# Reciprocal square roots of two normalisations on GpSimd (power) instead of ScalarE root and VectorE reciprocal

## What is computed

```python
def attn(x):                       # 16 heads of 32
    qf, kf = fft(x @ W_q.T per head), fft(x @ W_kv.T per head)
    qf, kf = qf / norm(qf), kf / norm(kf)      # norm of a head's 32 complex numbers
    v = real(ifft(qf * cumsum(kf, over rows)))
    return v @ W_o.T
x = x + attn(layernorm(x))
z = layernorm(x)
g = silu(z @ gate_w(fp8) * gate_scale) * (z @ up_w(fp8) * up_scale)    # 1536 wide
x = x + (g @ down_w(fp8)) * down_scale
```

## Time and profile before

| what | value |
|---|---|
| median of 3 runs | 439.82 us |
| profiled execution, its own time | 439.65 us |
| its span (first to last instruction) | 437.8 us |
| outside the span | 1.85 us |
| TensorE (PE) busy | 425.1 us, 97% |
| VectorE (DVE) busy | 276.2 us, 63% |
| ScalarE (ACT) busy | 185.2 us, 42% |
| GpSimd (POOL) busy | 104.9 us, 24% |

### The profile page before, as it was taken

The page is one execution under the profiler, slowest core; times in us unless marked ns, Lnnn a source line. Parts: engine busy times, 40 slices in busy tenths (PEclk is TensorE's granted clock), DMA queues, the critical chain, the costliest instruction groups (busy, mean ns, idle before and its releaser), DMA issues.

```text
span 437.8 us, 5468 instructions
## 1 busy us (share of the span) xinstructions
PE 425.1 (97%) x1976; PEld 280.2 (64%) x1976; DVE 276.2 (63%) x488; ACT 185.2 (42%) x299; POOL 104.9 (24%) x107
## 2 busy tenths in 40 slices
PE   4999999999999999999999999999999999999995
PEld 4886678745665676665565767666566666555554
DVE  5899889988797882347684571536865754523134
ACT  4958446873434542236432252434523243213130
POOL 0406620011745010400563311400254200400002
PEclk9999999999999999999999999999999999999999
DMA  7993490010240000250000100140000000200002
GB/s 215 328 293 117 141 304 4 0 49 2 72 155 15 1 2 0 85 156 0 2 0 2 49 1 1 47 146 0 0 2 1 1 0 1 96 1 1 0 0 97
DMA packets 17595, 26.14 MB, mean 60 GB/s; under 512 B 1824, under 2 KB 8224, under 8 KB 17568
## 3 DMA queue, kind: packets, MB, share of 16 engines
q1 hardware_dynamic: 17280, 25.77, 18.2%
q10 hardware_dynamic: 288, 0.02, 0.0%
HBM read 21.57 MB, written 4.19 MB: 59 GB/s over the span
## 4 chain that ended last, share of the span: by engine, by line
PE 93%; DMA 2%; POOL 2%; ACT 1%; DVE 1%; issue 0%; SPq 0%; DVEq 0%; POOLq 0%
PE bd L383 20%; PE bg L367 19%; PE bu L367 19%; PE ba L290 15%; PE ba L324 8%; PE bd L290 3%; PE ba L333 1%; PE bd L324 1%; PE ba L303 1%; PE ba L312 1%; DMA hT<-w_q_dram 1%; DMA xTr<-xT_dram 1%; PE bd L276 1%; PE bu L290 1%; PE bg L290 1%; POOL xTs L1350 1%
## 5 line engine op out<-in xcount | busy, mean ns | idle before, releaser
L383 PE MATMUL bd<-dw,fu 128*128 128x512 f32 x376 | 98.6, 406 | 0.0
L367 PE MATMUL bg<-hT,gu 128*128 128x512 f16 x384 | 91.1, 380 | 0.0
L367 PE MATMUL bu<-hT,gu 128*128 128x512 f16 x384 | 90.7, 379 | 0.0
L383 PEld LDWEIGHTS bd<-dw,fu 128*128 128x128 f32 x376 | 69.8, 188 | 16.1
L1046 DVE SCALAR_TENSOR_TENSOR ff<-bu,us,sl 128x512 f32<-128x512 f32 x48 | 35.9, 749 | 61.8 <-PE bu L367 59.8
L290 PE MATMUL ba<-wf,xTs 128*128 128x512 f32 x288 | 69.5, 395 | 0.0
L645 ACT ACTIVATE sl<-bg,gs 128x512 f32<-128x512 f32 x48 | 33.0, 688 | 80.4 <-PE bg L367 80.2
L367 PEld LDWEIGHTS bu<-hT,gu 128*128 128x128 f16 x384 | 37.6, 98 | 45.3
L367 PEld LDWEIGHTS bg<-hT,gu 128*128 128x128 f16 x384 | 34.9, 98 | 44.6 <-issue 8.4
L290 PEld LDWEIGHTS ba<-wf,xTs 128*128 128x128 f32 x288 | 53.7, 188 | 11.8 <-POOL xTs L1350 0.3
L655 ACT ACTIVATE fu<-ff 128x512 fp32r<-128x512 f32 x47 | 29.4, 628 | 55.3 <-PE bd L383 33.9
(11 more groups left out here) (161 smaller groups left out, 474.0 us busy)
## 6 DMA issues: line engine op xcount, KB each, us to landing
h<-x_dram SPq DMA_DIRECT2D x16, 256.0 KB, 3.7
out_dram<-h SPq DMA_DIRECT2D x16, 256.0 KB, 2.3
xTr<-xT_dram SPq DMA_DIRECT2D x12, 256.0 KB, 4.0
hT<-w_q_dram SPq DMA_DIRECT2D x4, 256.0 KB, 4.5
gu<-w_kv_dram SPq DMA_DIRECT2D x4, 256.0 KB, 5.5
h<-xT_dram SPq DMA_DIRECT2D x4, 256.0 KB, 7.5
hT<-gate_w_dram SPq DMA_DIRECT2D x2, 512.0 KB, 6.1
hT<-up_w_dram SPq DMA_DIRECT2D x2, 512.0 KB, 4.9
```

Of the source, the lines that this page charges most:

```text
L367: m = e.matmul(bk[:, :], gu[:, c, 4 * w + k, col:col + P], hT[:, b % 2, part, k, :], start=k == 0 and part == 0, stop=k == KT - 1 and part ...
L383: m = e.matmul(bd[t][:, :], fu_at(n)[:, part, P * t:P * t + P], dw[:, i, :], start=i == 0 and part == 0, stop=i == NI - 1 and part == 1)
```

## The change

The root of ScalarE and the reciprocal of VectorE are taken out at both places, with their table loads. `pool_root1` and `pool_root2` on GpSimd raise `E` (33 numbers for each row tile) and `E2` (one number for each row tile) to a tile of constants, -0.5, with ALU.pow. The Newton step stays. `act_first_root` becomes `act_first`, which runs a Silu after the opening. The orders of all five engines are written anew, and the tenancy of PSUM banks stays as it was. The diff, cut: of the order lists the places that the prediction speaks of are shown.

```diff
@@ -485,55 +488,53 @@
                 pe_gate_up(e, b, 1)
                 if nxt < NB:
                     pe_qk(e, nxt, 2, 0)
-                pe_down(e, b * NI)
-                if nxt < NB:
                     pe_qk(e, nxt, 2, 1)
-                pe_gate_up(e, b, 2)
-                if nxt < NB:
                     pe_qk(e, nxt, 3, 0)
                     pe_qk(e, nxt, 3, 1)
+                pe_down(e, b * NI)
+                pe_gate_up(e, b, 2)
                 pe_gate_up(e, b, 3)
+                if nxt < NB:
+                    pe_tri(e, nxt, 0)
                 pe_down(e, b * NI + 1)
+                pe_down(e, b * NI + 2)
...
-                    pe_o(e, nxt, 2)
-                pe_down(e, b * NI + 6)
-                if nxt < NB:
-                    pe_pT(e, nxt, 3)
-                pe_down(e, b * NI + 7)
-                if nxt < NB:
                     pe_o(e, nxt, 3)
+                pe_gate_up(e, b, 10)
                 pe_down(e, b * NI + 8)
-                pe_gate_up(e, b, 10)
                 if nxt < NB:
                     pe_hT(e, nxt, 0)
+                pe_gate_up(e, b, 11)
+                if nxt < NB:
                     pe_hT(e, nxt, 1)
-                pe_gate_up(e, b, 11)
-                if nxt < NB:
                     pe_hT(e, nxt, 2)
...
@@ -581,18 +582,6 @@
                     e.wait_ge(s_hT, 4 * (b - 1) + t + 1)
             e.activation(qk[:, t, w, :], ba[i][:, :], ACT.Copy).then_inc(a_cp, 1)
 
-        def act_sqrt1(e, b, ts):
-            g = slice(ts[0], ts[-1] + 1)
-            piece = n1_of(b, ts[0])
-            e.wait_ge(v_n1, 8 * piece + 3)
-            e.activation(Q[:, g, :], E[:, g, :], ACT.Sqrt).then_inc(a_rt1, 1)
-
-        def act_sqrt2(e, b, ts):
-            g = slice(ts[0], ts[-1] + 1)
-            piece = n1_of(b, ts[0])
-            e.wait_ge(v_n2, 5 * piece + 1)
-            e.activation(E2[:, 1, g], E2[:, 0, g], ACT.Sqrt).then_inc(a_rt2, 1)
-
         def act_ks(e, b, t):
             if b > 0 and t > 0:
                 e.wait_ge(p_carry, 3 * (b - 1) + t)
...
@@ -661,9 +650,9 @@
                 e.wait_ge(*rounded(n - 4))
             e.activation(part_at(half, n), stage_at(n), ACT.Abs, scale=0.5, saturate=False).then_inc(a_half, 1)
 
-        def act_first_root(e):
+        def act_first(e):
             e.wait_ge(v_one, 1)
-            e.activation(Q[:, 0, 1:2], Q[:, 0, 0:1], ACT.Sqrt)
+            e.activation(Q[:, 0, 1:2], Q[:, 0, 0:1], ACT.Silu)
 
         def act_minus(e):
             e.wait_ge(d_cst, 16)
@@ -686,16 +675,14 @@
             act_center(e, 0)
             act_center(e, 1)
             act_center(e, 2)
-            act_first_root(e)
             act_center(e, 3)
...
             act_qk(e, 0, 3, 1)
             act_wo_high(e, 0)
+            act_wo_high(e, 1)
             act_x(e, 1, 0)
-            act_sqrt1(e, 0, [2, 3])
-            act_x(e, 1, 1)
             act_pT(e, 0, 0)
             act_wo_low(e, 0)
-            act_wo_high(e, 1)
             act_wo_high(e, 2)
+            act_wo_low(e, 1)
             act_wo_high(e, 3)
-            act_wo_low(e, 1)
             act_wo_low(e, 2)
             act_wo_low(e, 3)
             act_ks(e, 0, 2)
+            act_x(e, 1, 1)
+            act_x(e, 1, 2)
+            act_ks(e, 0, 3)
             act_pT(e, 0, 1)
-            act_ks(e, 0, 3)
-            act_x(e, 1, 2)
             act_x(e, 1, 3)
+            act_first(e)
...
@@ -819,71 +802,69 @@
                 if nxt < NB:
                     act_qk(e, nxt, 0, 1)
                     act_qk(e, nxt, 1, 0)
-                act_silu(e, b * NI + 1)
-                if nxt < NB:
                     act_qk(e, nxt, 1, 1)
                     act_qk(e, nxt, 2, 0)
+                act_silu(e, b * NI + 1)
+                if nxt < NB:
                     act_qk(e, nxt, 2, 1)
+                    act_qk(e, nxt, 3, 0)
+                    act_qk(e, nxt, 3, 1)
+                act_fu(e, b * NI + 1)
                 act_silu(e, b * NI + 2)
-                act_fu(e, b * NI + 1)
-                if nxt < NB:
-                    act_qk(e, nxt, 3, 0)
-                act_fu(e, b * NI + 2)
-                act_silu(e, b * NI + 3)
...
@@ -942,30 +923,28 @@
             e.tensor_tensor(E[:, g, 1:33], S[:, g, :], rv[:, g].unsqueeze(2).broadcast_to([P, n, 32]),
                             ALU.mult).then_inc(v_n1, 1)
 
-        def dve_refine(e, sem_, at, e_ap, q_ap, y_ap, a_ap, out_ap):
-
-            e.reciprocal(y_ap, q_ap).then_inc(sem_, 1)
+        def dve_refine(e, sem_, at, e_ap, y_ap, a_ap, out_ap):
+
+            e.scalar_tensor_tensor(out=a_ap, in0=y_ap, scalar=-0.5, in1=y_ap, op0=ALU.mult, op1=ALU.mult).then_inc(sem_, 1)
             e.wait_ge(sem_, at + 1)
-            e.scalar_tensor_tensor(out=a_ap, in0=y_ap, scalar=-0.5, in1=y_ap, op0=ALU.mult, op1=ALU.mult).then_inc(sem_, 1)
+            e.tensor_tensor(a_ap, a_ap, e_ap, ALU.mult).then_inc(sem_, 1)
             e.wait_ge(sem_, at + 2)
-            e.tensor_tensor(a_ap, a_ap, e_ap, ALU.mult).then_inc(sem_, 1)
-            e.wait_ge(sem_, at + 3)
             e.scalar_tensor_tensor(out=out_ap, in0=a_ap, scalar=1.5, in1=y_ap, op0=ALU.add, op1=ALU.mult).then_inc(sem_, 1)
 
         def dve_norm_tail(e, b, ts):
             g, n = slice(ts[0], ts[-1] + 1), len(ts)
             piece = n1_of(b, ts[0])
-            at = 8 * piece
-            e.wait_ge(a_rt1, piece + 1)
-            dve_refine(e, v_n1, at + 3, E[:, g, :], Q[:, g, :], y0[:, g, :], Q[:, g, :], E[:, g, :])
-            e.wait_ge(v_n1, at + 7)
+            at = 7 * piece
+            e.wait_ge(p_rt1, piece + 1)
+            dve_refine(e, v_n1, at + 3, E[:, g, :], y0[:, g, :], Q[:, g, :], E[:, g, :])
...
@@ -1016,13 +995,13 @@
         def dve_ln2_tail(e, b, ts):
             g = slice(ts[0], ts[-1] + 1)
             piece = n1_of(b, ts[0])
-            e.wait_ge(a_rt2, piece + 1)
-            dve_refine(e, v_n2, 5 * piece + 1, E2[:, 0, g], E2[:, 1, g], E2[:, 2, g], E2[:, 3, g], E2[:, 4, g])
+            e.wait_ge(p_rt2, piece + 1)
+            dve_refine(e, v_n2, 4 * piece + 1, E2[:, 0, g], E2[:, 1, g], E2[:, 2, g], E2[:, 3, g])
 
         def dve_hn(e, b, t):
-            e.wait_ge(v_n2, 5 * n1_of(b, t) + 5)
+            e.wait_ge(v_n2, 4 * n1_of(b, t) + 4)
...
@@ -1087,20 +1066,19 @@
             dve_aggr_w(e, 2)
             dve_stats_w(e, 3)
             dve_less_w(e, 2)
+            dve_aggr_w(e, 3)
+            dve_less_w(e, 3)
             dve_stats_w(e, 4)
-            dve_aggr_w(e, 3)
-            dve_one(e)
             dve_aggr_w(e, 4)
             dve_stats_w(e, 5)
-            dve_less_w(e, 3)
-            dve_stats_w(e, 6)
             dve_aggr_w(e, 5)
             dve_less_w(e, 4)
+            dve_stats_w(e, 6)
             dve_aggr_w(e, 6)
             dve_less_w(e, 5)
-            dve_less_w(e, 6)
             dve_stats_w(e, 7)
             dve_aggr_w(e, 7)
+            dve_less_w(e, 6)
             dve_less_w(e, 7)
             dve_wf(e, 0, 0)
...
-                dve_f(e, b * NI + 2)
-                dve_fu(e, b * NI + 1)
-                if nxt < NB:
                     dve_sum(e, nxt, 2, 1)
-                dve_fu(e, b * NI + 2)
-                if nxt < NB:
-                    dve_stats1(e, nxt, 2)
                     dve_stats1(e, nxt, 3)
                     dve_sum(e, nxt, 3, 0)
                     dve_sum(e, nxt, 3, 1)
                     dve_norm_head(e, nxt, range(NT))
-                dve_f(e, b * NI + 3)
-                if nxt < NB:
                     dve_norm_tail(e, nxt, range(NT))
                     dve_scale(e, nxt, 0, 1)
+                dve_f(e, b * NI + 2)
+                dve_fu(e, b * NI + 1)
+                if nxt < NB:
+                    dve_scale(e, nxt, 1, 1)
                     dve_scale(e, nxt, 0, 0)
+                dve_fu(e, b * NI + 2)
...
                 dve_f(e, b * NI + 9)
                 if nxt < NB:
                     dve_o(e, nxt, 3)
                     dve_ln2_head(e, nxt, range(NT))
+                dve_fu(e, b * NI + 8)
+                dve_fu(e, b * NI + 9)
+                if nxt < NB:
                     dve_ln2_tail(e, nxt, range(NT))
                     dve_hn(e, nxt, 0)
+                dve_f(e, b * NI + 10)
+                if nxt < NB:
+                    dve_hT(e, nxt, 0)
+                dve_fu(e, b * NI + 10)
+                if nxt < NB:
                     dve_hn(e, nxt, 1)
...
@@ -1370,6 +1347,23 @@
             e.wait_ge(p_im, n + 1)
             e.tensor_copy(slot_0(qn), slot_0(buf[:, 0, :])).then_inc(p_z, 1)
 
+        def pool_exponent(e):
+            e.memset(less_half[:, :], -0.5).then_inc(p_exp, 1)
+
+        def pool_root1(e, b, ts):
+            g = slice(ts[0], ts[-1] + 1)
+            e.wait_ge(v_n1, 7 * n1_of(b, ts[0]) + 3)
+            e.wait_ge(p_exp, 1)
+            n = len(ts)
+            e.tensor_tensor(y0[:, g, :], E[:, g, :], less_half[:, :].unsqueeze(2).broadcast_to([P, n, 33]), ALU.pow).then_inc(p_rt1, 1)
+
```

(60 more changed lines are left out.)

435 lines of the change are left out of this document (213 added, 222 removed).

## The result

The changed kernel takes 526.38 us (median of 4 runs, 523.88 to 527.65) where the kernel before, beside it on the same chip, takes 439.50: 1.197 times as long, with a 95% interval of 1.193 to 1.202. The forecast was 439.3 with a range up to 443.5. The profiled execution took 526.7 us, 524.8 of it the span, 87.0 more than before.

The account below looks back on a forecast made before the run. TensorE, busy 97% of the span and never idle from 62 to 432 us, was taken as the bound. From 439.65 us only the opening's 0.4 came off, other terms 0: 439.3, range 438.7 to 440.2, outer ends 437.8 and 443.5.

Parts of the forecast that it names:

- The price of the power: GpSimd's power estimated at 1.85 us for 132 numbers, 0.9 for 66, 0.3 for 4; upper bound 5.3 for 132.
- the second piece: Block 0's first normalisation, tiles 2 and 3: VectorE work ahead of the tail covers 1.5 us; counted at nothing.
- The slack: First normalisation, blocks 2 and 3: a power up to 2.1 us is hidden before TensorE waits for `dve_f`.
- The triangle next in line: Blocks 2 and 3, one gate-up after the `dve_f` wait: its `ks` hides a power up to 2.6 us.
- Block 0's first piece: First normalisation in block 0: a power of 66 numbers is hidden up to 1.4 us.
- Block 1: First normalisation there has more room than blocks 2 and 3, as gate-up rounds without projections follow; no size given.
- The long power: Rival, 22%: the first normalisation's power outlasts 2.1 us and stops TensorE; 441.9 us, or 447 at the upper bound.
- The opening: Start-up: the table load leaves, TensorE's 0.97 us wait for the fourth centring goes; gain taken as 0.4 us.
- The second normalisation: Blocks 2 and 3, before the `hT` transposes: chain 0.5 us later, loss 0 to 0.3 us each, taken as 0.
- Moved transfers: SP's `sp_weights(7)` waits for the last W_o matmul ahead of xT(1,3): 0 to 0.5 us, taken as 0.
- Table loads: Sign to look for on ScalarE: table loads go down to two.
- The lock: Rival, 8%: GpSimd's power holds VectorE's `dve_fu` through the shared port, in blocks 2 and 3; 441.2 us.

Follow-up runs that it names:

- the half powers: Changed kernel with the first normalisation's power on 17 of each 33 numbers, the rest left at a constant: 485.6 us (one run).
- the place tried first: Kernel before with only the second normalisation's root as a short GpSimd power, ahead of `pool_x(b+2, 1)`: 445.30 us, ratio 1.0118.
- the orders alone: Changed kernel with a plain multiply by a constant in place of both powers, same engine and orders, roots left out: 440.34 us, ratio 1.0006.
- under 1 in the other: Kernel before with only the second normalisation's root as a short GpSimd power, behind `pool_x(b+2, 1)`: 440.53 us, ratio 1.0016.

## Why the prediction was wrong, point by point

**The price of the power** is the step of the prediction that failed: "two such functions make twelve times 3.2 ns, 5.1 + 0.2 = 5.3 us for 132 numbers" was called an upper bound, and 1.85 us was taken. It is 21.42 us, 4.0 times the bound and 11.6 times the estimate; 10.92 instead of 0.9 for 66; 1.0 to 1.3 instead of 0.3 for 4. The bound carried the ratio of VectorE's reciprocal to VectorE's product over to GpSimd. Nothing in the trace said that this ratio holds on another engine, so the row bounded nothing. The lower end was off as well, the other way: 0.56 us for a plain instruction on 132 numbers, where the product takes 0.41. With the right price, the prediction's own slacks give 3 x (21.4 - 2.1) + (10.9 - 1.4), and with the measured 9.7 for the second piece, which had no slack given, 77.1 us of stops and 516.4 us; the 10.3 us still missing to 526.7 are about what the lower clock added.

**The slack was right.** It said 2.1 us in front of `dve_f`; it measures 21.43 - 19.23 = 2.2, and 2.2 at half the size. The triangle next in line, at 2.6, was named too, and came up when `dve_f` was moved, at 2.3. Block 0's first piece: 1.4 said, 10.92 - 9.2 = 1.7 measured. The second piece has 10.91 - 9.7 = 1.2; the prediction named what stands behind that power, `pool_x` and the product that `pe_pT` needs, and then counted it at nothing without a number. Block 1 was said to have more room: 21.4 - 18.2 = 3.2.

**The long power as a rival** had the right place, the right wait and the right point of turning, and 22%. Its price stopped at the false bound, 447 us, and so the range and the chances of the other cases were too narrow.

**The clock** was in no term. Five stops of 9 to 19 us come with 10.7 us of longer matmuls, and five of 4 to 9 us, with the half powers, with 11.5.

**The opening**, 0.4 us taken: the wait for the fourth centring did go, and the fold of W_kv starts at 11.32 instead of 12.47. All of that and more is lost again, and the first projection came at 16.94, not 15.5. TensorE waits for VectorE's centring instead:

```profile
13.02 2.67 POOL L1327 TENSOR_TENSOR xTs<-h,xTs 128x512 fp32r<-128x512 f32 x2 [0.87 <-ACT xTs L563]
13.17 2.80 DVE L885 TENSOR_SCALAR gu<-gu,wmv 128x512 f32<-128x512 f32 x2
...
14.62 1.16 PE L279 MATMUL bd<-cst,gu 128*128 128x128 f32 x8 [0.97 <-DVE gu L885]
```

The third group's centring, late as the prediction had it, meets a GpSimd product and takes 2.80 us for two instead of 0.45 each. The prediction knew both the new place and the hold, and did not put the two together. The start of the first projection also differs between executions with the same opening order: 15.70 to 16.44 in five profiles with the old one (15.96 in the earlier trace rows), 16.00 to 16.98 in six with the new one. So the term has the wrong sign if it has any, and its 0.4 us are below what one profile can confirm.

**The second normalisation** at 0 to 0.3 us: nothing stops there in the changed kernel, whose order has `pool_x(b+2, 1)` ahead. The term is right for this order, and 5.4 us wrong for the place tried first. **Moved transfers** at 0: right, since the orders alone make no difference. **Table loads**: two are left, as said. **The lock**: no `dve_fu` is held by a power; what holds VectorE are plain GpSimd instructions. **The chances**: "its lower third, under 438.94" is nearer a sixth, 0.24 of the 1.5 us from 438.7 to 440.2; it changes none of the above.

## What to carry to other kernels

An operation that an engine has in no row has no upper bound from another engine's rows: work out the price at which the place breaks (here 2.1 us), and ask for one measurement of the operation by itself, since the places and the slacks in the sum were right. Where a stop has been caused by one late value, look for the second reader in the queue before moving the first. And count a waiting instruction by what stands behind it, on its own queue and through the transfers that this work releases: a 1.03 us power cost 5.4 us in one place and under 1 in the other.
